# Attention's lead-in moved into the block that computes the projections, in key-chunk order, on one core

## The chip, the cores and the metric

The kernel runs on one core of a Trainium2 chip. The metric is the device time in microseconds (us) of one execution; the time before is the median of three runs. A core has five engines that work side by side: TensorE (PE in the profile; its weight loads are listed as PEld), VectorE (DVE), ScalarE (ACT), GpSimd (POOL) and SyncE (SP), which here only issues DMAs. Each engine works through its own instructions in order and waits on semaphores for the others.

## The reference, cut to what matters

The layer is an attention with a convolutional side path, a layer norm, a linear layer with fake-quantised (MXFP4) operands, and a second layer norm, on two sequences of 2048 rows of 256 features, all in float32. The change touches only the scores and what feeds them:

```python
# D, H, DK = 256, 16, 16 ; batch 2, length 2048
q_in = linear(x, Wq_w, Wq_b).transpose(0, 2, 1)
Q3 = conv1d(q_in, convq_w, convq_b, (1, 1))                 # 3 taps
Q_cat = jnp.concatenate([q_in, Q3], axis=1).transpose(0, 2, 1)
Q = linear(Q_cat, qproj_w, qproj_b)                         # 16 heads of 16; K likewise
V = linear(x, Wv_w, Wv_b)
tau = sigmoid(conv1d(gelu(conv1d(x_conv, tau1_w, tau1_b, groups=D)), tau2_w, tau2_b))
delta = ...                                                 # the same, with del1, del2
scores = einsum('bhqd,bhkd->bhqk', Q, K) / sqrt(DK)
scores = scores * tau[..., None] + delta[:, :, None, :]
attn = jax.nn.softmax(scores, axis=-1)
out = einsum('bhqk,bhkd->bhqd', attn, V)
x = layernorm(x + linear(out, out_w, out_b))
x = layernorm(x + quantised_linear(x))
```

## The kernel before, in words

The program has two blocks, one after the other; an engine enters the second block only when every engine has finished the first.

**First block: projections.** The 2 x 2048 rows are cut into eight chunks of 512 (`NCHUNK`, chunks 0 to 7). For each chunk, TensorE computes the keys (two halves `o` of 128 features, `project(n, 1, o)`, 18 matmuls each), half of the values (`values`, 12 matmuls), the queries of half 0, the other half of the values, the queries of half 1, and the pointwise convolution of the next chunk (`pointwise`, 8 matmuls, which the trace shows as 16). VectorE does the convolution taps of the next chunk, the low parts of the split of each float32 number into two, the bias of the values and the scaling of the queries with tau; ScalarE does the high parts, the GELUs and sigmoids. SyncE stores queries, keys and delta to DRAM (`k_parts`, `q_parts`, `delta_parts`). Four heads form a group; in chunks 1 to 4 SyncE also loads chunk 0 to 3 of the first group's keys and queries back into `k_set` and `q_set` (`group_load`, 14 DMAs each, semaphore `group_loaded`). It does so at its place in its queue, behind the loads of `tau_r` and ahead of the stores of the chunk's keys.

**Second block: attention.** There are 32 iterations (`NIT`): 8 groups of four heads by 4 chunks of 512 queries. An iteration needs the maximum of each query row before its softmax, and these maxima are computed one iteration ahead. They are cut into 32 units (`UNITS`): a unit is one pair of matmuls (`s_unit`, line 205) of 128 queries by 512 keys, one in each half of the array, and one VectorE reduction over the pair (`max_unit`, line 215). The units alternate between two pairs of PSUM banks, so unit s may only start on TensorE when the reduction of unit s-2 is done. When the 32 units of iteration j are done, VectorE reduces them to `nm` (line 1009), GpSimd splits `nm` in two parts, three units later TensorE transposes them (item "rows", line 800), VectorE copies them to `nm_rows` (line 998), and SyncE writes them as two extra rows into `q_set` (`rows_store`, line 785). Then the scores of iteration j are computed again, transposed, with the maximum already subtracted (`st`, line 813), ScalarE exponentiates them (line 967), and TensorE multiplies by the values (`pv_half`, line 826). The list `items` holds all units and rows in order; in steady state one slot of TensorE is one pair at line 813, eight matmuls at line 826 and mostly one item at line 205.

Before its first `st`, TensorE has to be 45 items into that list (`lead_in`): the 32 units of iteration 0, its rows item, and 12 units of iteration 1. `PRE_STEP` says how many items are done already in the first block, by chunk and by one of seven places in a chunk: 28 (`PRE`). Places 0 and 1 lie behind the key projections, 2 behind the first half of the values, 3 behind the queries of half 0, 4 behind the second half of the values, 5 behind the queries of half 1, and 6 behind the pointwise convolution. VectorE has the same seven places in its own order (`pre_max`). The other 17 items stand at the head of the second block (line 896), each followed by six matmuls whose result nobody reads (`WARM`, line 901), 102 in all.

At the end of the first block SyncE waits for the last stores and group loads (lines 334 to 337). At the start of the second, ScalarE loads the table of the exponential and GpSimd fills `v_grp`, the values of the first group.

## Time and profile before

| | |
|---|---|
| time before, median of 3 runs | 1717.49 us (1715.56 to 1720.35) |
| profiled execution: time, span of the trace | 1709.64 us, 1707.8 us |
| first block | 0 to 254.2 us |
| lead-in at the head of the second block | 254.2 to 274.4 us |
| busy: TensorE, VectorE, ScalarE, GpSimd | 96%, 90%, 78%, 4% of the span |
| granted TensorE clock, mean | 0.982 |

Times in the trace are us from the start of the span. "x" counts instructions. A bracket at the end of a timeline row is the idle time of that engine just before the row, and the instruction that ended it. PEclk is the granted TensorE clock as a share of full speed: 1.00 is 2.4 GHz, 0.50 is 1.2 GHz. Rows of a timeline that merge several instructions give the start of the first and the time to the end of the last. The ends of matmuls are modelled, so a TensorE that is 100% busy may hide short idle stretches.

### The profile page before, as it was taken

To read this page: it belongs to the slowest core of one execution; us is meant where nothing else is said; L and a number is where in the kernel's file an instruction comes from. 1 tells how busy PE (TensorE), PEld (TensorE's weight loads), DVE (VectorE), ACT (ScalarE), POOL (GpSimd) and SP (SyncE) were. 2 spreads that over 40 slices of the span, in tenths; PEclk is the share of its full clock that TensorE was granted. 3 is DMA by queue.
4 is the path that set the end of the run, shared out by engine and by line. 5 is a ranking of instruction groups with operands and counts; after the bars stand their busy time and mean duration, and the time that the engine had idled before them with its cause. 6 is when DMAs were issued, how large, how long until landed. Compare 5 with 4: busy or idle time off the path is not lost.

```text
span 1707.8 us, 33648 instructions
## 1 busy us (share of the span) xinstructions
PE 1639.0 (96%) x13978; PEld 742.4 (43%) x13978; DVE 1536.4 (90%) x1622; ACT 1325.2 (78%) x2401; POOL 74.5 (4%) x133
## 2 busy tenths in 40 slices
PE   8999989999999999999999999999999999999775
PEld 7677754333333333333333333333333333334564
DVE  5688978999999999999999999999999999973896
ACT  3788724888888888888888888888888888886333
POOL 3000002000000000000000000000000000010110
PEclk9999999999999999999999999999999999999988
DMA  3377336000600060023004100602060000002331
GB/s 110 99 183 185 106 95 91 8 8 8 83 8 9 13 78 12 10 35 57 8 8 61 34 8 8 85 9 82 8 84 8 8 8 15 8 10 55 104 123 50
DMA packets 46960, 84.72 MB, mean 50 GB/s; under 512 B 9116, under 2 KB 21020, under 8 KB 44092
## 3 DMA queue, kind: packets, MB, share of 16 engines
q1 hardware_dynamic: 44952, 82.49, 22.6%
q8 instruction: 109, 1.79, 0.5%
q14 instruction: 43, 0.35, 0.1%
q10 hardware_dynamic: 1856, 0.09, 0.1%
HBM read 51.36 MB, written 30.67 MB: 48 GB/s over the span
## 4 chain that ended last, share of the span: by engine, by line
PE 61%; DVE 22%; ACT 2%; issue 1%; ACTq 0%; POOL 0%; DVEq 0%
PE ps L826 26%; PE ps L813 20%; DVE mx L215 17%; PE ps L205 11%; PE ps L885 1%; DVE work L1052 1%; ACT y L944 1%; PE ps L901 1%; ACT o_sb L944 1%; DVE small L1047 0%; PE ps L800 0%; PE ps L891 0%; DVE stats L1026 0%; PE ps L857 0%; DVE work L1061 0%
## 5 line engine op out<-in xcount | busy, mean ns | idle before, releaser
L215 DVE TENSOR_REDUCE mx<-ps 128x2 f32<-128x1024 f32 x1024 | 1233.0, 1223 | 58.8 <-PE ps L205 49.2
L967 ACT ACTIVATE e<-ps 128x512 f32<-128x512 f32 x2048 | 1110.1, 596 | 198.7 <-PE ps L813 158.5
L826 PE MATMUL ps<-e,v_grp 128*32 128x256 f32 x8192 | 655.1, 392 | 0.5 <-ACT ev L956 0.5
L813 PE MATMUL ps<-q,k 52*128 52x512 f32 x2048 | 523.8, 497 | 3.8 <-ACT e L967 3.8
L205 PE MATMUL ps<-k,q 50*128 50x512 f32 x2048 | 420.0, 402 | 10.9 <-DVE mx L215 6.2
L813 PEld LDWEIGHTS ps<-q,k 52*128 52x128 f32 x2048 | 198.9, 183 | 429.0 <-ACT e L967 399.6
L826 PEld LDWEIGHTS ps<-e,v_grp 128*32 128x32 f32 x8192 | 161.5, 108 | 358.6 <-issue 199.4
L205 PEld LDWEIGHTS ps<-k,q 50*128 50x128 f32 x2048 | 198.0, 187 | 39.1 <-DVE mx L215 30.4
L605 PE MATMUL ps<-x_p,m_p 128*128 128x512 f32 x576 | 141.3, 401 | 0.0
L605 PEld LDWEIGHTS ps<-x_p,m_p 128*128 128x128 f32 x576 | 107.7, 190 | 30.6 <-issue 5.7
L437 DVE SCALAR_TENSOR_TENSOR hid<-x_c,dw_w,hid 128x512 f32<-128x512 f32 x128 | 88.5, 747 | 13.2 <-ACT hid L379 13.2
L385 ACT ACTIVATE hid<-hid 128x512 f32<-128x512 f32 x64 | 40.5, 632 | 41.0 <-DVE hid L437 39.5
L1026 DVE BATCH_NORM_STATS2 stats<-ps 128x6 f32<-128x256 f32 x64 | 23.2, 418 | 27.9 <-PE ps L857 18.8
L379 ACT ACTIVATE hid<-x_c,dw_b,dw_w 128x512 f32<-128x512 f32 x64 | 46.7, 804 | 0.2
L83 POOL CAST nm_pad<-nm 128x16 fp32r<-128x16 f32 x32 | 6.3, 197 | 914.9 <-DVE nm L1009 914.9
L944 ACT ACTIVATE y<-ps,shift,rstd 128x256 f32<-128x256 f32 x32 | 15.4, 563 | 24.3 <-DVE shift L1038 19.7
L857 PE MATMUL ps<-wo_t,v_all 128*128 128x256 f32 x128 | 34.2, 392 | 0.0
L883 PE MATMUL ps<-bias,ones 128*128 128x512 bf16 x16 | 8.3, 521 | 25.9 <-ACT o_sb L944 25.9
L944 ACT ACTIVATE o_sb<-ps,shift,rstd 128x256 f32<-128x256 f32 x32 | 15.4, 563 | 21.1 <-DVE shift L1038 21.1
L625 PE MATMUL ps<-hid,pw_w 128*16 128x512 f32 x128 | 31.2, 594 | 0.5 <-ACT hid L385 0.5
L428 ACT ACTIVATE q_sp<-qx 128x512 fp32r<-128x512 f32 x16 | 10.1, 630 | 26.3 <-DVE qx L465 26.2
L616 PE MATMUL ps<-wv_p,x_p 128*128 128x256 f32 x192 | 27.1, 292 | 2.0 <-DVE v_all L455 2.0
(117 smaller groups left out, 658.2 us busy)
## 6 DMA issues: line engine op xcount, KB each, us to landing
k<-k_parts SPq DMA_DIRECT2D x42, 256.0 KB
q<-q_parts SPq DMA_DIRECT2D x42, 256.0 KB
k_parts<-k_sp SPq DMA_DIRECT2D x16, 512.0 KB, 4.9
q_parts<-q_sp SPq DMA_DIRECT2D x16, 512.0 KB, 4.5
att<-ev SPq DMA_DIRECT2D x32, 256.0 KB
x_c<-in_x_t SPq DMA_DIRECT2D x8, 514.0 KB, 6.4
tau_r<-tau_rows SPq DMA_DIRECT2D x16, 256.0 KB
x_in<-in_x SPq DMA_DIRECT2D x8, 512.0 KB, 3.7
```

The lines of the kernel that those rows point to most:

```text
L205: last = nc.tensor.matmul(ps[:, s_bank(s) + half, :], q_set[r, g % 2, jh, lo + qt * P:lo + (qt + 1) * P], k_set[r, g % 2, jh, kc * CH:(kc ...
L215: nc.vector.tensor_reduce(mx[:, j % 2, :, jh, qt, kc], ps[:, b0:b0 + 2, :], AX.X, ALU.max).then_inc(s_free, 1)
L379: nc.scalar.activation(hid[:, k, c, r], x_c[:, n % 2, c, 1:1 + CH], ACT.Identity, bias=dw_b[:, k, c, r:r + 1], scale=dw_w[:, k, c, r, 1:2] ...
L385: nc.scalar.activation(hid[:, k, c, r], hid[:, k, c, r], ACT.Gelu).then_inc(gelu_done, 1)
L437: nc.vector.scalar_tensor_tensor(y_, x_c[:, n % 2, c, which:which + CH], dw_w[:, k, c, r, which:which + 1], y_, ALU.mult, ALU.add).then_in ...
L605: last = nc.tensor.matmul(ps[:, o, :], m_p[:, kw, side, c, tap, P * o:P * (o + 1)], x_p[:, n % 2, kx_, c, tap:tap + CH], start=(m == 0), s ...
L625: last = nc.tensor.matmul(ps[32 * k:32 * k + H, TD_BANK, :], pw_w[:, k, 2 * c + r, :], hid[:, k, c, r, :], start=(j < 2), stop=(j >= 6))
L813: nc.tensor.matmul(ps[:, st_bank(n), :], k_set[r, g % 2, jh, kt * P:(kt + 1) * P], q_set[r, g % 2, jh, lo:lo + CH], start=True, stop=True) ...
L826: last = nc.tensor.matmul(ps[32 * h:32 * (h + 1), 0, PVW * part:PVW * (part + 1)], v_grp[:, kt, h, :], e[:, x % E_BUFS, h * CH + PVW * par ...
L857: last = nc.tensor.matmul(dst, a_t[p][:, c, P * a:P * (a + 1)], wo_t[:, c, :], start=False, stop=(c == CT - 1))
L944: last = nc.scalar.activation(dst[:, a], tok(bank0, a), ACT.Identity, scale=rstd[:, k, p, a:a + 1], bias=shift[:, k, p, a:a + 1])
L967: nc.scalar.activation(e[:, x % E_BUFS, h * CH:(h + 1) * CH], ps[:, st_bank(n), :], ACT.Exp).then_inc(e_ready, 1)
```

## The change

All 45 items of the lead-in are now done in the first block. `PRE_STEP` gives 4 items to chunk 1 (places 3 to 6, one each), 5 each to chunks 2 to 6 (places 2 to 6), and 16 to chunk 7 (2, 2, 3, 2, 2, 2, 3). The 32 units of iteration 0 are taken in another order: by key chunk first (`place_of`), so that the first 8 need only the first key chunk; the first unit of each key chunk waits for that chunk's 14 loads. The last unit of iteration 0, `nm` and the rows item fall into chunk 7: `row_maxima`, `split_max` and `rows_store` become functions shared by both blocks and are called for iteration 0 in the first. `rows_store(sp, 0)` stands in SyncE's queue of chunk 7 behind the key stores and ahead of the delta store. The 102 matmuls at line 901 are gone. SyncE's waits for the last stores move from the end of the first block to the start of the second, ahead of the loads that follow there. The buffers that these stores read (`q_sp`, `k_sp`, `td`, `d_sp`) are allocated first, so that only buffers loaded behind these waits lie over them. The zeroing of `nm_pad` moves from VectorE to GpSimd's start.

```diff
+        def place_of(j, u):
+            if j == 0:
+                return u % (HH * TT) // HH, u % HH, u // (HH * TT)
+            return u // (HH * NQ), u // NQ % HH, u % NQ
 
         def s_unit(pe, s):
             if s >= 2:
                 pe.wait_ge(s_free, s - 1)
             g, lo = j // NQ, j % NQ * CH
-            if u == 0 and j % NQ == 0:
+            qt, jh, kc = place_of(j, u)
+            if j == 0 and (qt, jh) == (0, 0):
+                pe.wait_ge(group_loaded, 16 * GROUP_DMAS * (kc + 1))
+            if u == 0 and j % NQ == 0 and j > 0:
                 pe.wait_ge(group_loaded, loads_of(g + 1))
-            qt, jh, kc = u // (HH * NQ), u // NQ % HH, u % NQ
...
+        def rows_turn(pe, s):
+            j, u = items[s]
+            pe.wait_ge(s_free, s - 1)
+            pe.wait_ge(nm_ready, j + 1)
+            nc.tensor.transpose(ps[:, s_bank(s), 0:P], nm_pad[:].bitcast(F32), ident_f[:]).then_inc(s_full, 1)
...
-        PRE_STEP = {4: (0, 0, 0, 0, 0, 0, 2), 5: (0, 0, 1, 1, 1, 1, 1), 6: (0, 0, 1, 1, 1, 1, 1), 7: (2, 2, 2, 2, 2, 2, 4)}
+        PRE_STEP = {1: (0, 0, 0, 1, 1, 1, 1)} | {n: (0, 0, 1, 1, 1, 1, 1) for n in range(2, 7)} | {7: (2, 2, 3, 2, 2, 2, 3)}
...
+                        if n > 1:
+                            sp.wait_ge(group_loaded, 16 * GROUP_DMAS * (n - 1))
                         group_load(sp, 0, group_loaded, slice((n - 1) * CH, n * CH))
                     for o in range(CT):
                         sp.wait_ge(k_split, CT * n + o + 1)
                         store_parts(k_parts, k_sp, n, o, k_stored)
+                    if n == NCHUNK - 1:
+                        rows_store(sp, 0)
...
-                sp.wait_ge(k_stored, 16 * CT * NCHUNK)
-                sp.wait_ge(q_stored, 16 * CT * NCHUNK)
-                sp.wait_ge(d_stored, 16 * NCHUNK)
-                sp.wait_ge(group_loaded, loads_of(1))
...
                     for s in range(PRE, lead_in):
                         s_item(s)
-                        for m in range(WARM):
-                            for half in range(2):
-                                r = rows_of(half, K_S)
-                                nc.tensor.matmul(ps[:, st_bank(half), :], q_set[r, 0, 0, 0:P], k_set[r, 0, 0, 0:CH], start=True, stop=True)
...
+                    sp.wait_ge(k_stored, 16 * CT * NCHUNK)
+                    sp.wait_ge(q_stored, 16 * CT * NCHUNK)
+                    sp.wait_ge(d_stored, 16 * NCHUNK)
                     sp.dma_start(fw[:], t["ffn_w"].rearrange("(a p) i -> p a i", p=P)).then_inc(ffn_loaded, 16)
...
-                    rows_store(sp, 0)
```

TensorE in chunk 1, from its key projections to its pointwise convolution. In the rows of before, line 605 is a projection, 616 the values, 625 the pointwise convolution; `ps` is PSUM. Before:

```order
L605 MATMUL ps<-x_p,m_p 128x512 x36
L616 MATMUL ps<-wv_p,x_p 128x256 x12
L605 MATMUL ps<-x_p,m_p 128x512 x18
L616 MATMUL ps<-wv_p,x_p 128x256 x12
L605 MATMUL ps<-x_p,m_p 128x512 x18
L625 MATMUL ps<-hid,pw_w 16x512 x8
```

TensorE at the same place now; there the same three are lines 668, 679 and 688, and line 218 is the pair of a unit:

```order
L668 MATMUL ps<-x_p,m_p 128x512 x36
L679 MATMUL ps<-wv_p,x_p 128x256 x12
L668 MATMUL ps<-x_p,m_p 128x512 x18
L218 MATMUL ps<-k,q 128x512 x2
L679 MATMUL ps<-wv_p,x_p 128x256 x12
L218 MATMUL ps<-k,q 128x512 x2
L668 MATMUL ps<-x_p,m_p 128x512 x18
L218 MATMUL ps<-k,q 128x512 x2
L688 MATMUL ps<-hid,pw_w 16x512 x8
L218 MATMUL ps<-k,q 128x512 x2
```

Four units stand in chunk 1 where none stood; the first of them, behind the 18 matmuls of the queries of half 0, is the one that waits for the first 14 loads. TensorE from the first half of the values in chunk 7 to the start of the second block, before (line 205 is a unit's pair, line 901 the unread matmuls, the two branches are the border of the blocks):

```order
L616 MATMUL ps<-wv_p,x_p 128x256 x12
L205 MATMUL ps<-k,q 128x512 x4
L605 MATMUL ps<-x_p,m_p 128x512 x18
L205 MATMUL ps<-k,q 128x512 x4
L616 MATMUL ps<-wv_p,x_p 128x256 x12
L205 MATMUL ps<-k,q 128x512 x4
L605 MATMUL ps<-x_p,m_p 128x512 x18
L205 MATMUL ps<-k,q 128x512 x12
L288 UNCONDITIONAL_BRANCH
L789 UNCONDITIONAL_BRANCH
L205 MATMUL ps<-k,q 128x512 x2
L901 MATMUL ps<-k,q 128x512 x6
```

TensorE at the same place now; line 235 is the transpose of the rows item, line 859 the first scores of attention proper (line 813 before):

```order
L679 MATMUL ps<-wv_p,x_p 128x256 x12
L218 MATMUL ps<-k,q 128x512 x4
L235 MATMUL ps<-ident_f,nm_pad 128x128
L668 MATMUL ps<-x_p,m_p 128x512 x18
L218 MATMUL ps<-k,q 128x512 x4
L679 MATMUL ps<-wv_p,x_p 128x256 x12
L218 MATMUL ps<-k,q 128x512 x4
L668 MATMUL ps<-x_p,m_p 128x512 x18
L218 MATMUL ps<-k,q 128x512 x10
L343 UNCONDITIONAL_BRANCH
L837 UNCONDITIONAL_BRANCH
L859 MATMUL ps<-q,k 128x512 x8
```

The transpose stands ahead of the queries of half 0, and behind the border attention's own matmuls come first.

## Rows read from the trace of the kernel before

**Rows 1.** the profile page, part 1: busy time, share of the span, instructions.
```profile
PE 1639.0 (96%) x13978; PEld 742.4 (43%) x13978; DVE 1536.4 (90%) x1622; ACT 1325.2 (78%) x2401; POOL 74.5 (4%) x133
```

**Rows 2.** the chain that ended last, in order of time: start us, us, what.
```profile
254.24 0.79 PE ps L205 x2
...
274.45 0.59 ACT e L967
```

**Rows 3.** groups by line, 254.2 to 274.05 us: busy us, mean ns, idle before.
```profile
L215 DVE TENSOR_REDUCE mx<-ps 128x2 f32<-128x1024 f32 x16 | 18.6, 1218 | 1.8 <-PE ps L205 1.8
L901 PE MATMUL ps<-k,q 50*128 50x512 f32 x102 | 16.0, 420 | 0.0
```

**Rows 4.** busy time by stretch, chunks 4 and 6: PE, PEld, DVE, ACT, POOL, PEclk, DMA.
```profile
142.62:166.62 24.00, 24.00 (x118) 17.37 (x116) 18.88 (x31) 19.97 (x30) 0.00 (x0) 1.00 0.68 179
...
192.78:218.85 26.07, 26.07 (x124) 18.03 (x122) 24.03 (x32) 19.05 (x27) 0.00 (x0) 1.00 0.34 105
```

**Rows 5.** timeline of the ScalarE queue at the start of the second block.
```profile
254.20 1.28 ACT L967 ACT_TABLE_LOAD   x1 [5.95 <-PEq L288]
```

**Rows 6.** timeline of TensorE: where chunks 2 and 3 begin.
```profile
95.88 8.65 PE L605 MATMUL ps<-x_p,m_p 128*128 128x512 f32 x36
...
119.23 8.67 PE L605 MATMUL ps<-x_p,m_p 128*128 128x512 f32 x36
```

**Rows 7.** timeline of TensorE in chunk 1.
```profile
82.42 4.37 PE L605 MATMUL ps<-x_p,m_p 128*128 128x512 f32 x18
86.62 1.58 PE L616 MATMUL ps<-wv_p,x_p 128*128 128x256 f32 x12
```

**Rows 8.** timeline of SyncE's DMA issues in chunk 1.
```profile
88.90 0.28 SPq L166 DMA_DIRECT2D k<-delta_parts  x1
89.22 0.89 SPq L293 DMA_DIRECT2D k_parts<-k_sp  x2
```

**Rows 9.** DMA issues of 220 to 262 us.
```profile
delta_parts<-d_sp SPq DMA_DIRECT2D x1, 64.0 KB, 1.9
```

**Rows 10.** DMA issues of 84 to 90 us: count, KB, median us to landing.
```profile
k_parts<-k_sp SPq DMA_DIRECT2D x2, 512.0 KB, 5.6
```

**Rows 11.** timeline of TensorE after its idle stretch at 56 us.
```profile
57.68 2.93 PE L616 MATMUL ps<-wv_p,x_p 128*128 128x256 f32 x12 [1.98 <-DVE v_all L455]
```

**Rows 12.** timeline of VectorE in chunk 7, and the reduction to `nm`.
```profile
232.53 2.35 DVE L215 TENSOR_REDUCE mx<-ps 128x2 f32<-128x1024 f32 x2
...
248.89 4.61 DVE L215 TENSOR_REDUCE mx<-ps 128x2 f32<-128x1024 f32 x4
...
260.68 0.22 DVE L1009 TENSOR_REDUCE nm<-mx 128x16 f32<-128x64 f32 x1
```

**Rows 13.** timeline of TensorE in chunk 7.
```profile
231.29 0.50 PE L205 MATMUL ps<-k,q 50*128 50x512 f32 x2 [0.17 <-DVE mx L215]
231.73 4.47 PE L605 MATMUL ps<-x_p,m_p 128*128 128x512 f32 x18
```

**Rows 14.** waits of SyncE's queue, 240 to 260 us: us in total, times, longest.
```profile
SPq L337 <- DMA q_parts<-q_sp: 4.3, 1, 4.3
```

**Rows 15.** busy time by stretch, 280 to 282 us.
```profile
280.00:282.00 2.00, 2.00 (x14) 0.66 (x14) 1.06 (x2) 1.08 (x2) 0.00 (x0) 0.55 1.02 127
```

**Rows 16.** timeline of TensorE as attention gets going.
```profile
277.47 0.64 PE L826 MATMUL ps<-e,v_grp 128*32 128x256 f32 x8
...
282.64 0.64 PE L826 MATMUL ps<-e,v_grp 128*32 128x256 f32 x8
...
283.88 0.64 PE L826 MATMUL ps<-e,v_grp 128*32 128x256 f32 x8
```

**Rows 17.** timeline of VectorE: the first tap of chunk 6's round.
```profile
195.62 2.87 DVE L437 SCALAR_TENSOR_TENSOR hid<-x_c,dw_w,hid 128x512 f32<-128x512 f32 x4 [1.51 <-ACT hid L379]
```

**Rows 18.** timeline of ScalarE: four middles, and the end of that round.
```profile
194.77 2.94 ACT L379 ACTIVATE hid<-x_c,dw_b,dw_w 128x512 f32<-128x512 f32 x4
...
220.16 0.68 ACT L408 ACTIVATE td<-ps,pw_b 16x512 f32<-16x512 f32 x1
```

More of the change, by code:

```diff
@@ L212, in max_unit, with rows_copy, row_maxima, split_max @@
             dve.wait_ge(s_full, s + 1)
-            qt, jh, kc = u // (HH * NQ), u // NQ % HH, u % NQ
+            qt, jh, kc = place_of(j, u)
             b0 = s_bank(s)
             nc.vector.tensor_reduce(mx[:, j % 2, :, jh, qt, kc], ps[:, b0:b0 + 2, :], AX.X, ALU.max).then_inc(s_free, 1)
+        def rows_turn(pe, s):
[3 more added lines that the diff above has]
+            nc.tensor.transpose(ps[:, s_bank(s), 0:P], nm_pad[:].bitcast(F32), ident_f[:]).then_inc(s_full, 1)
+        def rows_copy(dve, s):
+            j, u = items[s]
+            dve.wait_ge(s_full, s + 1)
+            if j > 0:
+                dve.wait_ge(rows_set, j * ROWS_INC)
+            nc.vector.tensor_copy(nm_rows[:], ps[0:2 * HG * TT, s_bank(s), 0:P]).then_inc(s_free, 1)
+        def row_maxima(dve, s):
+            j, u = items[s]
+            dve.wait_ge(s_free, s + 1)
+            if j > 0:
+                dve.wait_ge(nm_ready, j)
+            nc.vector.tensor_reduce(nm[:], mx[:, j % 2].rearrange("p a j q c -> p (a j q) c"), AX.X, ALU.max, negate=True).then_inc(nm_max, 1)
+        def split_max(pool, j):
+            pool.wait_ge(nm_max, j + 1)
+            if j > 0:
+                pool.wait_ge(s_full, rows_at[j - 1] + 1)
+            cols = nm[:].rearrange("p (h q) -> p h q", h=HG)
+            high(nc.gpsimd, nm_parts[:, :, 0], cols).then_inc(nm_high, 1)
+            pool.wait_ge(nm_high, j + 1)
+            low(nc.gpsimd, nm_parts[:, :, 1], cols, nm_parts[:, :, 0]).then_inc(nm_ready, 1)
+        def rows_store(sp, j):
+            sp.wait_ge(s_free, rows_at[j] + 1)
+            g, lo = j // NQ, j % NQ * CH
+            for h in range(HG):
+                row = HALF * (h // HH) + ROW_MAX
+                sp.dma_start(q_set[row:row + 2, g % 2, h % HH, lo:lo + CH].bitcast(F32).rearrange("t (a l) -> t a l", a=TT),
+                             nm_rows[h * 2 * TT:(h + 1) * 2 * TT, :].bitcast(F32)).then_inc(rows_set, 16)
         early = top.enter_context(ExitStack())
+        q_sp = sb(early, "q_sp", [P, CT, 2, CH], F32R)
+        k_sp = sb(early, "k_sp", [P, CT, 2, CH], F32R)
+        td = sb(early, "td", [48, CH])
+        d_sp = sb(early, "d_sp", [48, 2, CH], F32R)
         x_c = sb(early, "x_c", [P, 2, CT, CH + TAPS - 1])
@@ L342, in _ @@
                 nc.gpsimd.memset(eps_col[:], EPS).then_inc(ident_ready, 1)
+                nc.gpsimd.memset(nm_pad[:].bitcast(F32), 0.0).then_inc(pad_zero, 1)
                 pool.wait_ge(ident_ready, 2)
@@ L530, in pre_max @@
                     for s in pre_at.get((n, place), ()):
+                        j, u = items[s]
+                        if u == "rows":
+                            rows_copy(dve, s)
+                            continue
                         max_unit(dve, s)
+                        if u == UNITS - 1:
+                            row_maxima(dve, s)
                 for n in range(NCHUNK):
@@ L630, in pre_scores @@
                     for s in pre_at.get((n, place), ()):
-                        s_unit(pe, s)
+                        if items[s][1] == "rows":
+                            rows_turn(pe, s)
+                        else:
+                            s_unit(pe, s)
                 beta(1, 0)
@@ L794, in s_item @@
                         j, u = items[s]
[L795 removed]
+                        if u == "rows":
+                            rows_turn(pe, s)
+                        else:
                             s_unit(pe, s)
[L797 to L800 removed]
                     def st(x, jh):
```

56 lines of the change are left out of this document (11 added, 45 removed).

## The prediction, made before the changed kernel had run

> **What bounds the kernel now.** I read the page first: TensorE is busy for 96% of the span [rows 1], so whatever takes or gives TensorE time counts unless it lies where TensorE waits. Then the chain that ended last, in order of time. From the border of the blocks it runs through the lead-in on TensorE, and 20.2 us later (254.24 to 274.45) it reaches the first exponential [rows 2]: until then nothing of attention proper is done, ScalarE stands still. The groups by line of that stretch show what fills it: 16 reductions on VectorE of 18.6 us together, and 102 unread matmuls on TensorE [rows 3]. So the lead-in is paced by both, and all of it is on the path. Last I read the first block, to which the work goes, by stretches: in chunks 4 and 6 TensorE is busy 24.00 of 24.00 and 26.07 of 26.07 us [rows 4]. TensorE bounds that block as well, and nothing moved there is free.
>
> **What goes.** With the change the second block begins with the exponential's table load of 1.28 us (254.20 to 255.48) [rows 5], beside which the first scores run; the first exponential follows at 1.3 us behind the border instead of 20.2. Removed: 18.9 us.
>
> **What the units cost in chunks 1 to 6.** A chunk without units takes 119.23 - 95.88 = 23.35 us [rows 6]; chunk 6, with five single units, 26.07, or (26.07 - 23.35) / 5 = 0.54 us a unit; chunk 4, with two units side by side, 24.00 [rows 4]. Chunk 1 gets four single units, 2.2 us; chunks 2 and 3 five each, 2 x 2.72 = 5.4; chunk 4 goes from 24.00 to 26.07, 2.1; chunks 5 and 6 are as they were. Sum 9.7 us. From below, if each cost what one of the side-by-side pair does ((24.00 - 23.35) / 2 = 0.33), chunks 1 to 3 would come to 4.6 instead of 7.6; I take the single units' price, since they stand singly. VectorE, busy for 24.03 us of chunk 6, just holds that pace; if it doesn't, that is a rival below.
>
> **The new wait in chunk 1.** This is the largest term. The first unit stands behind the queries of half 0, which end at 82.42 + 4.37 = 86.79 us; before, TensorE went straight on to the values [rows 7]. The unit waits for all 14 loads of the first key chunk. SyncE issues them at the same place as before, and nothing ahead of them changes: the last is issued at 88.90 us, 2.1 us after TensorE has arrived, and the stores of the keys follow it at once [rows 8]. When it lands the trace does not print. From below, a small transfer on a quiet queue takes 1.9 us [rows 9]: 88.90 + 0.28 + 1.9 = 91.1, a wait of 4.3 us. From above, the key stores issued from 89.22 on take 5.6 us [rows 10]; if the loads have to share the queues with them to the end, the last lands with them at 89.7 + 5.6 = 95.3, a wait of 8.5 us. I take the 5.6 us of the transfers right behind, from the last load's own issue: 88.90 + 5.6 = 94.5, a wait of 7.7 us, because the load is in the same queues in the same microseconds. Behind the waiting unit are queued the second half of the values, the queries of half 1, the pointwise convolution and all of chunk 2; VectorE waits in its turn behind the same unit with the bias of the values, four taps and the query scaling behind it. TensorE has no slack to give this back, so it stays on the path. The three later waits of this kind find their loads landed: the second key chunk is first read at the end of chunk 2, its loads are issued some ten us earlier.
>
> The Trainium skill (page "DMA: Bandwidth & Descriptors", section "Anatomy of one DMA — SWDGE (gpsimd) path") puts a transfer at a fixed 2.0 us plus its bytes over the bandwidth. For a transfer alone the trace agrees (1.9 us) [rows 9]; on the loaded queue it does not (5.6 us) [rows 10]. By that rule the wait would be about 4 us and not 7.7, which is the rival of the early landing below.
>
> **The clock.** After a standstill TensorE works at half speed for a while: behind an idle stretch of 1.98 us that ends at 57.68, the 12 matmuls of the values took 2.93 us [rows 11] instead of 1.58 [rows 7]. I expect the same behind the wait in chunk 1. For some 3.4 us at 1.2 GHz half is lost, 1.7 us; bounds 0 and 3.4.
>
> **Chunk 7.** It is paced by VectorE and by the two bank pairs. It loses one reduction: the last four start at 248.89 and take 4.61 us, 1.14 us apiece [rows 12]. It gains the reduction to `nm`, 0.22 us [rows 12], and the copy of the rows, an estimate of as much again. But the rows item stands ahead of the queries of half 0 and may start only when the unit two before it is reduced. That unit is the first of place 2, whose reduction VectorE begins at 232.53 and ends 1.2 us later (two took 2.35); with `nm` ahead, 234.0 [rows 12]. Before, the queries of half 0 began at 231.73, having waited 0.17 us [rows 13]; now they begin behind the transpose at about 234.4. From there VectorE follows TensorE (it waits for the units after each projection), so all shifts by 2.7 and the missing reduction takes back 1.1: +1.6 us. Bounds: -0.7 (only VectorE's own sum counts) and +3.
>
> **The border.** SyncE waited 4.3 us for the last query stores at the end of the first block [rows 14]; that ended with VectorE's last reduction (248.89 + 4.61 = 253.50), so removing it gives nothing by itself. Behind the border it delays only loads that nobody needs for tens of us. `rows_store` is issued in chunk 7, more than 10 us ahead of the first scores, and is off the path. GpSimd's `v_grp` is filled beside the first exponentials.
>
> **The start of attention.** Before, the first slots of attention ran partly at 1.2 GHz as well: the granted clock was 0.55 at 280 to 282 us [rows 15], and from 277.47 to 282.64 three slots took 5.17 us, where the next took 1.24 [rows 16]; that is 1.45 us above three normal ones. Now the unread matmuls are gone, and attention starts at 1.2 GHz out of the thin end of chunk 7. I take the same loss, 0 in the difference; bounds -1.4 (the clock is up before the first values) and +1.5 (twice as long low). From then on the 32 iterations are the same instructions.
>
> **The sum.** Added 9.7 + 7.7 + 1.7 + 1.6 = 20.7 us, removed 18.9: +1.8 us. On the profiled execution's 1709.64 us (span 1707.8) that is 1711.4. This execution lies 7.85 us below the median of the runs shown, so I add the difference to the median: 1717.49 + 1.8 = 1719.3 us. The gain is eaten up in the first block, mostly by one wait.
>
> **Rivals.**
> 1. *The early landing.* The loads arrive by 91.1 us, the wait is 4.3 us and the clock costs 0.9: 9.7 + 4.3 + 0.9 + 1.6 - 18.9 = -2.4, 1715.1 us. For it: the loads are issued ahead of the key stores, and the 1.9 us [rows 9]. Against it: the 5.6 us [rows 10].
> 2. *VectorE and ScalarE become the bound of chunks 2 to 4 (the slower side).* A round of them goes from the first tap of a chunk to the next: in chunk 6 from 195.62 [rows 17] to the end of the sigmoids, 220.16 + 0.68 = 220.84 [rows 18], and one ScalarE middle of 0.7 us more (four took 2.94): 25.9 us, against TensorE's 26.07. There is 0.1 us of slack, without group loads and without the extra border columns that chunks 3 and 4 have. It decides from a round longer than 26.1 us; at 27.5 us it adds 1.4 in each of chunks 2, 3 and 4: +1.8 + 4.2 = +6.0, 1723.5 us. Against it: most of the extra border work is under 0.2 us an instruction, and slack of earlier chunks has to be used up first.
> 3. *Little of it shows.* The loads land early (4.3), the clock does not fall in chunk 1, chunk 7 costs -0.7, and attention starts at full clock (-1.4): 9.7 + 4.3 - 0.7 - 1.4 - 18.9 = -7.0, 1710.5 us, faster. The wait can't be less than 2.1 us, as the last load is issued only then.
>
> **Chances.** Forecast 0.52, rival 1 0.20, rival 2 0.18, rival 3 0.10. A change of 0.3% is 5.2 us; less than that a measurement of this kernel can't tell from none. Rival 3 and a tenth of rival 1 are faster: 0.12. Rival 2 and a ninth of the forecast (a wait at its upper bound with a long clock loss) are slower: 0.24. The rest, 0.64, is no change. The range of 8 in 10 takes in rivals 1 and 2 and stops short of rival 3: 1712.5 to 1726 us.
>
> **What would show it.** Right: in chunk 1 the first pair of a unit on TensorE has an idle stretch of 7 to 8 us before it, ended by a DMA, and half-speed matmuls behind it; chunks 2, 3 and 4 take 26 us each; the queries of half 0 in chunk 7 begin 2 to 3 us late; the border of the blocks comes at about 275 us instead of 254.2; the first exponential 1.3 us behind it; the iterations take as long as before. Wrong: an idle stretch in chunk 1 of 4 us or less (rival 1), chunks 2 to 4 of 27 us or more with VectorE fully busy (rival 2), or a wait at the head of the second block for the rows, for `v_grp` or for the clock.

## The result, and the profile after

The changed kernel takes 1720.93 us (median of 20 runs, 1716.02 to 1735.77), the kernel before 1715.7 us in the same comparison (20 runs, 1709.92 to 1726.52). The ratio is 1.0046 (95% interval 1.0028 to 1.0065), which is 7.9 us more (4.8 to 11.2); the two medians alone are 5.2 us apart. The time lies in the predicted range and 1.6 us from the predicted one. But the step was forecast at +1.8 us, inside what a measurement can tell from nothing, and it is about three times that by the medians and four times by the ratio: a slower kernel, if by half a percent. That the absolute time came so close is partly luck: the forecast stood on the median of three runs, 1717.49 us, and over 20 runs the kernel before has 1715.7. The profiled executions took 1716.65 and 1709.64 us, 7.0 us apart (spans 1714.9 and 1707.8 us), and it is in them that the difference is followed below. Both lie near the lowest time of their kernel.

The first part of the page of the changed kernel, as [rows 1] of before:

```profile
PE 1635.2 (95%) x13876; PEld 735.6 (43%) x13876; DVE 1534.8 (89%) x1621; ACT 1324.4 (77%) x2401; POOL 74.5 (4%) x134
```

Here TensorE is busy for 3.8 us less with 102 instructions less, in a span that is 7.0 us longer. So the time isn't in added work but in standstills and in the speed of the clock.

The timeline of TensorE of the changed kernel, in chunk 1, in chunk 7 and at the start of attention (start us, us, instruction, count, idle before and what ended it):

```profile
82.30 4.37 PE L668 MATMUL ps<-x_p,m_p 128*128 128x512 f32 x18
94.15 0.80 PE L218 MATMUL ps<-k,q 50*128 50x512 f32 x2 [7.48 <-DMA k<-delta_parts]
94.88 2.93 PE L679 MATMUL ps<-wv_p,x_p 128*128 128x256 f32 x12
...
98.46 5.46 PE L668 MATMUL ps<-x_p,m_p 128*128 128x512 f32 x18
...
253.90 0.33 PE L235 MATMUL ps<-ident_f,nm_pad 128*128 128x128 f32 x1 [2.01 <-DVE mx L228]
253.98 6.01 PE L668 MATMUL ps<-x_p,m_p 128*128 128x512 f32 x18
...
276.49 1.19 PE L859 MATMUL ps<-q,k 52*128 52x512 f32 x3 [1.74 <-PEq L343]
...
281.08 1.08 PE L872 MATMUL ps<-e,v_grp 128*32 128x256 f32 x8
...
283.24 1.08 PE L872 MATMUL ps<-e,v_grp 128*32 128x256 f32 x8
...
285.40 1.08 PE L872 MATMUL ps<-e,v_grp 128*32 128x256 f32 x8
...
287.56 1.02 PE L872 MATMUL ps<-e,v_grp 128*32 128x256 f32 x8
...
289.18 0.64 PE L872 MATMUL ps<-e,v_grp 128*32 128x256 f32 x8
```

In chunk 1, where the values followed at once on the queries [rows 7], TensorE now stands still for 7.48 us, and the values and the queries behind it take 2.93 and 5.46 us instead of 1.58 and 4.37: the granted clock is 0.50 from 90.4 to 100.7 us, over all of the values and the first part of the queries. In chunk 7 the transpose waits 2.01 us for VectorE, where 0.17 us stood [rows 13], and the queries behind it take 6.01 us instead of 4.47. Behind the border, a slot of attention at first takes 2.16 us (it begins at 281.08, 283.24, 285.40 and 287.56), and from 289.18 us on the normal 1.24.

Chunks 2, 3 and 4 and attention's first slots by stretch (us, busy TensorE, weight loads, VectorE, ScalarE, GpSimd, granted clock, DMA share, GB/s); they answer to [rows 4, 15]:

```profile
108.26:134.34 26.08, 26.08 (x124) 18.03 (x122) 24.06 (x31) 18.46 (x26) 0.00 (x0) 1.00 0.58 149
134.34:160.46 26.12, 26.12 (x124) 18.04 (x123) 24.07 (x36) 19.12 (x29) 0.00 (x0) 1.00 0.62 156
160.46:186.53 26.07, 26.07 (x124) 18.02 (x123) 24.10 (x36) 19.15 (x29) 0.00 (x0) 1.00 0.58 156
...
281.00:288.00 7.00, 7.00 (x44) 2.29 (x44) 2.78 (x3) 3.71 (x8) 2.88 (x7) 0.50 1.06 154
```

The three chunks are TensorE's alone, as chunk 6 was. The last row is the one to remember: TensorE is busy for 7.00 of 7.00 us as far as the profile shows, and its clock is 1.2 GHz all the same.

The timeline of SyncE of the changed kernel, the last of the 14 loads and the key stores behind it ([rows 8] before); then ScalarE's at the border ([rows 5]):

```profile
88.77 0.28 SPq L166 DMA_DIRECT2D k<-delta_parts  x1
89.09 0.89 SPq L348 DMA_DIRECT2D k_parts<-k_sp  x2
```

```profile
276.45 1.28 ACT L1009 ACT_TABLE_LOAD   x1 [4.40 <-PEq L343]
277.74 2.56 ACT L1009 ACTIVATE e<-ps 128x512 f32<-128x512 f32 x5
```

The loads are issued when they were, and reach the waiting unit 5.4 us later (88.77 to 94.15). The border lies at 276.45 us, and the first exponential 1.3 us behind it.

Last, a place that is the same in all these kernels and lies behind all that was changed: VectorE's reduction to `nm` for iteration 1, and for the last iteration. In the kernel before:

```profile
305.08 0.22 DVE L1009 TENSOR_REDUCE nm<-mx 128x16 f32<-128x64 f32 x1
...
1519.90 0.22 DVE L1009 TENSOR_REDUCE nm<-mx 128x16 f32<-128x64 f32 x1
```

and in the changed kernel:

```profile
310.39 0.22 DVE L251 TENSOR_REDUCE nm<-mx 128x16 f32<-128x64 f32 x1
...
1527.19 0.22 DVE L251 TENSOR_REDUCE nm<-mx 128x16 f32<-128x64 f32 x1
```

At the first the changed kernel is 5.31 us late, at the last 7.29. So 5.3 us arise ahead of 310 us and 2.0 in the 30 iterations that are the same instructions in both; behind them 0.3 us come back, which makes the 7.0.

### The profile page after: what moved, and what is told of

It reads as the page before. It is cut to its first block, busy times and chain, and to the rows that moved or that the text cites. A ratio compares the mean times of both kernels' runs of the same rounds, so it can differ in the third digit from the quotient of the medians.

```text
span 1714.9 us, 33445 instructions
## 1 busy us (share of the span) xinstructions
PE 1635.2 (95%) x13876; PEld 735.6 (43%) x13876; DVE 1534.8 (89%) x1621; ACT 1324.4 (77%) x2401; POOL 74.5 (4%) x134
## 4 chain that ended last, share of the span: by engine, by line
PE 60%; DVE 21%; ACT 2%; issue 1%; DMA 1%; SPq 0%; ACTq 0%; POOL 0%; DVEq 0%
PE ps L872 26%; PE ps L859 20%; DVE mx L228 17%; PE ps L218 11%; PE ps L903 1%; DMA out<-o_sb 1%; PE ps L931 0%; ACT y L986 0%; PE ps L235 0%; DVE stats L1061 0%; ACT o_sb L986 0%; DVE work L1087 0%; PE ps L901 0%; DVE small L1082 0%; PE ps L937 0%
## 5 line engine op out<-in xcount | busy, mean ns | idle before, releaser
L494 DVE SCALAR_TENSOR_TENSOR hid<-x_c,dw_w,hid 128x512 f32<-128x512 f32 x128 | 88.6, 747 | 10.2 <-ACT hid L436 10.2
L442 ACT ACTIVATE hid<-hid 128x512 f32<-128x512 f32 x64 | 40.5, 632 | 57.9 <-DVE hid L494 56.5
L1061 DVE BATCH_NORM_STATS2 stats<-ps 128x6 f32<-128x256 f32 x64 | 23.1, 417 | 27.4 <-PE ps L903 18.9
L981 ACT ACTIVATE std<-mv,eps_col 128x4 f32<-128x4 f32 x16 | 4.9, 305 | 33.2 <-DVE mv L1065 27.9
L903 PEld LDWEIGHTS ps<-wo_t,v_all 128*128 128x128 f32 x128 | 27.1, 212 | 4.6
```

Source lines behind the costliest of these rows:

```text
L442: nc.scalar.activation(hid[:, k, c, r], hid[:, k, c, r], ACT.Gelu).then_inc(gelu_done, 1)
L494: nc.vector.scalar_tensor_tensor(y_, x_c[:, n % 2, c, which:which + CH], dw_w[:, k, c, r, which:which + 1], y_, ALU.mult, ALU.add).then_in ...
L903: last = nc.tensor.matmul(dst, a_t[p][:, c, P * a:P * (a + 1)], wo_t[:, c, :], start=False, stop=(c == CT - 1))
```

## The experiments

Ratios are to the kernel before, run on the same chip (its medians there: 1713.98 to 1714.96 us). Three distances are read from every trace: from the start of the queries in chunk 1 (82.42 before, 82.30 after, 82.07 to 86.41 elsewhere, since the start of the kernel varies) to the border of the blocks; from the border to the `nm` of iteration 1; and the stretch of low clock that begins at most 10 us ahead of the border or behind it and lasts beyond it.

Each trace is one execution. The times of those of e5 and e9 lie 7 and 8 us above the median of their kernels; they and those of e4 and e8 have a further stretch of low clock of 20 to 31 us at the end of attention, behind all three distances.

| kernel | queries to border | border to `nm` | low clock there | ratio |
|---|---|---|---|---|
| before | 171.78 | 50.88 | 10.2, and 3.4 | 1 |
| changed | 194.15 | 33.94 | 17.1 | 1.0046 (1.0028 to 1.0065) |
| changed, again (e10) | 191.80 | 33.83 | 17.1 | 1.0050 (1.0024 to 1.0076) |
| e1 | 182.07 | 36.61 | 23.9 | 0.9994 (0.9972 to 1.0016) |
| e2 | 189.96 | 37.64 | 23.9 | 1.0044 (1.0016 to 1.0072) |
| e3 | 194.40 | 40.08 | 23.9 | 1.0029 (1.0000 to 1.0058) |
| e4, one run | 191.89 | 36.73 | 23.9 | 1726.56 us |
| e5 | 171.75 | 55.63 | 44.4 | 1.0027 (0.9996 to 1.0057) |
| e6 | 194.95 | 30.51 | none | 1.0015 (0.9987 to 1.0044) |
| e7 | 180.02 | 30.52 | none | 0.9938 (0.9914 to 0.9962) |
| e8, one run | 187.66 | 33.88 | 17.1 | 1721.97 us |
| e9 | 180.02 | 38.46 | 27.3 | 0.9972 (0.9952 to 0.9992) |

**No wait in chunk 1 (e1).** The four units of chunk 1 move: two to its end, one more each to chunks 2 and 3.

```diff
-PRE_STEP = {1: (0, 0, 0, 1, 1, 1, 1)} | {n: (0, 0, 1, 1, 1, 1, 1) for n in range(2, 7)} | {7: (2, 2, 3, 2, 2, 2, 3)}
+PRE_STEP = {1: (0, 0, 0, 0, 0, 0, 2)} | {n: (0, 1, 1, 1, 1, 1, 1) for n in (2, 3)} | {n: (0, 0, 1, 1, 1, 1, 1) for n in (4, 5, 6)} | {7: (2, 2, 3, 2, 2, 2, 3)}
```

> The four units of chunk 1 are moved: two to place 6 of chunk 1, where the loads have landed, one more each to chunks 2 and 3 (place 1). Theory (the wait for the first 14 loads and the clock behind it are lost outright, since TensorE bounds the first block): the idle stretch of 7.5 us in chunk 1 goes, no half-speed matmuls follow, chunks 2 and 3 become 26.6 us each, the border of the blocks comes 9 to 10 us earlier than in the changed kernel (near 267 us), and the time is 9 to 10 us below it, about 2 us below the kernel before (ratio 0.998 to 1.000). Rival A (VectorE and ScalarE bound the chunks with five or six units, slack 0.1 us): chunks 2 and 3 become 27.2 us or more, with TensorE idle in them, and the border comes only 8 us earlier. Rival B (what is lost in chunk 1 is slack that chunk 7 takes back): the border moves by less than 5 us.

Measured: 1712.86 us. The timeline of TensorE in chunk 1, then chunks 2 and 3 by stretch:

```profile
90.29 1.58 PE L679 MATMUL ps<-wv_p,x_p 128*128 128x256 f32 x12
91.70 4.37 PE L668 MATMUL ps<-x_p,m_p 128*128 128x512 f32 x18
```

```profile
100.21:126.92 26.71, 26.71 (x127) 18.14 (x125) 26.10 (x33) 18.54 (x27) 0.00 (x0) 1.00 0.59 149
126.92:153.68 26.76, 26.76 (x127) 18.14 (x125) 24.87 (x37) 18.87 (x29) 0.00 (x0) 1.00 0.62 153
```

No standstill, and values and queries at full speed. Chunk 1 takes 14.13 us from its queries to chunk 2, instead of 25.96; a sixth unit in chunks 2 and 3 costs 0.6 us each, though VectorE is busy for 26.10 us of chunk 2. The border comes 12.1 us earlier than in the changed kernel's first trace and 9.7 us earlier than in its second (e10); 1.5 us of the 12.1 lie in chunk 7, where e1 happens to keep full speed. 2.7 us are given back behind the border, where the clock stays low longer (23.9 us against 17.1). The wait is the largest single cost, as the forecast had it: the interval of e1's ratio lies below that of the changed kernel, and without the wait the kernel stands level with the one before.

**The rows item a place later (e2).** In chunk 7 the transpose comes behind the queries of half 0 instead of ahead of them.

```diff
-{7: (2, 2, 3, 2, 2, 2, 3)}
+{7: (2, 2, 2, 3, 2, 2, 3)}
```

> Only the rows item of chunk 7 moves, from place 2 (ahead of the queries of half 0) to place 3 (behind them). Theory: TensorE's idle 2.0 us before the transpose goes, and with it the half-speed stretch in the queries of half 0 (6.01 us against 4.47), so the queries of half 0 begin 2 us earlier and the border comes 3 to 4 us earlier than in the changed kernel (near 273 us). Rival: chunk 7 is paced by VectorE's sum, and the border moves by less than 1 us, with VectorE's idle time merely elsewhere. Time 3 us below the changed kernel or the same.

Measured: 1723.14 us. TensorE's timeline in chunk 7:

```profile
255.32 4.49 PE L668 MATMUL ps<-x_p,m_p 128*128 128x512 f32 x18
259.65 0.27 PE L235 MATMUL ps<-ident_f,nm_pad 128*128 128x128 f32 x1
```

The standstill of 2.01 us is gone, the queries keep full speed, and chunk 7 takes 34.14 us instead of 37.73. Against the changed kernel's second trace, where the queries kept full speed too (36.16 us, e10), the new place gives 2.0 us; the rest was the clock. The border is 4.2 us earlier (1.8 against e10), and `nm` comes 3.7 us later behind it, with 23.9 us of low clock instead of 17.1: in this execution the start of attention takes what chunk 7 gives. The time doesn't move. So the standstill was real, but removing it alone gained nothing that the runs show.

**What the unread matmuls did (e5, e3, e6).** In the kernel before alone (e5) the 102 unread matmuls are left out, and nothing else:

```diff
                     for s in range(PRE, lead_in):
                         s_item(s)
-                        for m in range(WARM):
-                            for half in range(2):
-                                r = rows_of(half, K_S)
-                                nc.tensor.matmul(ps[:, st_bank(half), :], q_set[r, 0, 0, 0:P], k_set[r, 0, 0, 0:CH], start=True, stop=True)
```

> The kernel before, with only its 102 unread matmuls taken out; the 17 items stay at the head of the second block. Theory (attention's own mix of matmuls at 1.2 GHz does not reliably bring the clock back; the unread matmuls did): the clock is still at 0.5 when the first scores of attention start, stays there for 10 to 20 us more, the slots of that stretch take 2.16 us instead of 1.24, and the kernel is 4 to 9 us slower than before (ratio 1.002 to 1.005). Rival (the late recovery in the changed kernel comes from starting attention right at the border, with its loads and GpSimd's work beside it): the clock comes back within 4 us as before, and since the unread matmuls also stood in the lead-in's way, the kernel is 0 to 2 us faster than before.

Measured: 1720.38 us, its ratio just not clear of 1. Its stretches behind the border:

```profile
258.00:277.00 19.00, 12.60 (x36) 5.04 (x36) 17.65 (x19) 1.10 (x1) 14.13 (x25) 0.50 0.47 88
277.00:297.00 20.00, 19.74 (x104) 6.82 (x101) 9.72 (x9) 11.64 (x22) 0.00 (x0) 0.52 0.99 116
```

The first row is the lead-in, the second attention: TensorE is busy for 19.74 of 20.00 us and at 0.52 of its clock. The way from the border to `nm` is 4.75 us longer than before. The low clock lasts from 252.0 to 296.4 us. In the kernel before it had begun in the thin end of chunk 7 as well, at 247.7 us, but it was over at 257.9, 3.7 us behind the border, and the next fall came only at 278.4, when the unread matmuls had ended. They brought the clock back and held it, and the change took them away together with the lead-in. The 4.75 us are a balance: the first exponential comes 0.9 us earlier without them (19.4 us behind the border instead of 20.2), and the way from it to `nm` is 5.6 us longer.

In e3 the changed kernel gets unread matmuls again where TensorE would wait: 17 pairs around the last three units of chunk 7, seven between the first scores of attention.

```diff
+                def fill(bank, pairs):
+                    for m in range(pairs):
+                        for half in range(2):
+                            r = rows_of(half, K_S)
+                            nc.tensor.matmul(ps[:, bank + half, :], q_set[r, 0, 0, 0:P], k_set[r, 0, 0, 0:CH], start=True, stop=True)
...
+                        if (n, place) == (NCHUNK - 1, 6):
+                            if k == 0:
+                                pe.wait_ge(v_evac, 2 * NCHUNK)
+                                pe.wait_ge(td_ready, NCHUNK)
+                            fill(V_BANK, (3, 2, 8)[k])
...
+                        if s == PRE - 1:
+                            fill(V_BANK, 4)
...
+                            if x < AHEAD and 2 <= n < HG * AHEAD - 1:
+                                for m in range(3 if n == 2 else 1):
+                                    for other in range(2):
+                                        r = rows_of(other, K_S)
+                                        nc.tensor.matmul(ps[:, 4 + other, :], q_set[r, 0, 0, 0:P], k_set[r, 0, 0, 0:CH], start=True, stop=True)
```

> Unread matmuls are put where TensorE idles: 17 pairs at the end of chunk 7 between the last units, 7 pairs between the first scores of attention. Nothing else changes. Theory (attention starts at 1.2 GHz because TensorE was thinly used before it): the granted clock stays at 1.0 from 270 us on, the first four slots of attention take 1.24 instead of 2.16 us, and steady state is reached 3 us earlier; the time is 3 us below the changed kernel. Rival (the slow start is the wait for the exponentials, not the clock): the slots stay above 1.8 us with the clock at 1.0, and nothing is gained. A loss of 1 us would mean that the unread matmuls stand in the way of the scores.

Measured: 1724.2 us. Its timeline of TensorE at the border, and the stretch behind it:

```profile
277.02 0.69 PE L872 MATMUL ps<-q,k 52*128 52x512 f32 x3 [1.11 <-PEq L343]
...
278.92 0.79 PE L872 MATMUL ps<-q,k 52*128 52x512 f32 x1 [0.52 <-ACT e L1027]
```

```profile
280.00:300.00 20.00, 20.00 (x115) 7.21 (x111) 8.99 (x8) 10.95 (x21) 11.05 (x20) 0.50 1.00 160
```

This fill held the clock until 1.6 us behind the border (278.6 us) and lost it there, behind a standstill of 1.11 us and within one of 0.52 us. Then TensorE is busy for 20.00 of 20.00 us at 1.2 GHz. The result is the longest way to `nm` of the changed kernels in one trace, 40.08 us; neither the theory nor its rival had that. Over all runs e3 is not slower than the changed kernel (1.0029 against 1.0046, intervals overlap). The Trainium skill (page "TensorE: Matmul & The Clock Gate", section "What's actually happening") has the throttled state as the default and "activity releases the throttle". By that rule a TensorE that is always busy should come to full speed; this row, 20.00 of 20.00 us busy by the profile at a granted clock of 0.50, does not agree with it.

In e6 the same places are filled denser: `(3, 2, 9)` and 7 pairs at the end of chunk 7, five pairs instead of three behind the third of the first scores.

```diff
-                            fill(V_BANK, (3, 2, 8)[k])
+                            fill(V_BANK, (3, 2, 9)[k])
-                            fill(V_BANK, 4)
+                            fill(V_BANK, 7)
-                                for m in range(3 if n == 2 else 1):
+                                for m in range(5 if n == 2 else 1):
```

> As the kernel e3_warm, with more unread matmuls: 21 pairs at the end of chunk 7 instead of 17, 9 pairs between the first scores instead of 7, the most of them in the 1.3 us in which ScalarE loads its table. Theory (in e3_warm the clock fell 1.7 us behind the border because TensorE stood still there for 1.1 and 0.5 us; once the slots start at 2.4 GHz they hold it): the clock stays at 1.0 through the start of attention, the first slots take 1.24 us, steady state is reached 4 to 5 us earlier than in the changed kernel, the time is 4 to 5 us below it, near the kernel before (ratio 0.999 to 1.002). Rival (the border's standstill alone brings the clock down): it falls again at the same place, and the start costs what it cost in e3_warm, 6 us more than in the changed kernel.

Measured: 1716.12 us. The stretch behind its border at 280.66 us:

```profile
281.00:293.00 12.00, 11.94 (x108) 5.35 (x104) 6.60 (x6) 11.11 (x21) 7.14 (x14) 1.00 0.81 158
```

Full clock, and 30.51 us to `nm`: 3.4 us less than in the changed kernel and 9.6 less than in e3, which differs from it by six pairs. A standstill of 0.42 us is left at its border, where e3 has 1.11. The ratios of the whole kernels, 1.0015 against 1.0046, point the same way, but their intervals overlap.

**What the loads of chunk 1 wait for (e4, e8).** The forecast had the last load share the queues with the key stores issued behind it. In e4 SyncE holds these stores until all 14 loads have landed.

```diff
+                    if n == 1:
+                        sp.wait_ge(group_loaded, 16 * GROUP_DMAS)
                     for o in range(CT):
                         sp.wait_ge(k_split, CT * n + o + 1)
                         store_parts(k_parts, k_sp, n, o, k_stored)
```

> SyncE holds back the key stores of chunk 1 until the 14 loads of the first key chunk have landed; nothing else changes. Theory as in the prediction (the loads share the queues with the 1 MB of key stores issued right behind them): the loads land near 91 us instead of 94.2, TensorE's idle stretch in chunk 1 shrinks from 7.5 to 4 or 5 us. Rival (the loads' own small rows and the loads of tau_r ahead of them take that long): the stretch stays at 7 us or more, and the key stores are issued only at 94 us.

Measured: 1726.56 us, one run. The last load and the first key store in SyncE's timeline, and TensorE's unit:

```profile
92.23 0.28 SPq L166 DMA_DIRECT2D k<-delta_parts  x1
98.37 0.89 SPq L348 DMA_DIRECT2D k_parts<-k_sp  x2
```

```profile
98.40 0.80 PE L218 MATMUL ps<-k,q 50*128 50x512 f32 x2 [8.18 <-DMA k<-delta_parts]
```

With nothing issued behind it, the last load is still there only 6.1 us after its issue (92.23 to 98.37, where SyncE's wait for it ends). The stores are not what makes it late: the rival named ahead of the run was right. In e8 the loads go ahead of the two loads of `tau_r` (256 KB each, a broadcast), which stood ahead of them:

```diff
-                    sp.wait_ge(tau_stored, 16 * (n + 1))
-                    if n > 0:
-                        sp.wait_ge(q_evac, CT * n)
-                    for o in range(CT):
...
-                        sp.dma_start(tau_r[:, o], src).then_inc(tau_loaded, 16)
                     if 0 < n <= NQ:
...
                         group_load(sp, 0, group_loaded, slice((n - 1) * CH, n * CH))
+                    sp.wait_ge(tau_stored, 16 * (n + 1))
+                    if n > 0:
+                        sp.wait_ge(q_evac, CT * n)
+                    for o in range(CT):
...
+                        sp.dma_start(tau_r[:, o], src).then_inc(tau_loaded, 16)
```

> The changed kernel, with SyncE's 14 loads put ahead of its wait for the tau rows and of the two loads of tau_r (in chunks 1 to 4). Theory (e4_late has shown that the key stores behind the loads do not delay them; what does is the 512 KB of tau_r ahead of them and their own 784 KB): the last load is issued 2 us earlier and lands 3.5 to 4.5 us behind its issue instead of 5.3, so TensorE's idle stretch in chunk 1 is 4 to 5 us instead of 7.5. Rival (the loads' own rows pile up on few of the 16 DMA engines, whatever is ahead): the landing stays 5 to 6 us behind the last issue, and the stretch shrinks by the 2 us of the earlier issue alone, to 5.5 us.

Measured: 1721.97 us, one run. SyncE's timeline and TensorE's:

```profile
89.36 0.28 SPq L166 DMA_DIRECT2D k<-delta_parts  x1
89.74 1.23 SPq L382 DMA_DIRECT2D tau_r<-tau_rows  x2
```

```profile
91.22 0.50 PE L218 MATMUL ps<-k,q 50*128 50x512 f32 x2 [2.33 <-DMA k<-delta_parts]
```

Now the last load is there 1.9 us after its issue, with the 512 KB of `tau_r` issued behind it, and TensorE waits 2.33 us; theory (4 to 5) and rival (5.5) both expected more. Of the 5.15 us less than in the changed kernel 1.6 are the earlier issue and 3.5 the faster landing. So in these two single executions the landing goes with what is in the queues ahead of the loads, not with what follows them. The border comes 187.66 us behind the queries, 4.1 to 6.5 us sooner than in the two runs of the changed kernel. The time of the whole is no verdict on it: it is one run, and it has a further low-clock stretch at the end of attention.

**All of it together (e7), and without the fill (e9).** e7 is the changed kernel with the edits of e1, e2 and e6; e9 is e7 without any unread matmul. Their edits are those shown above.

> Three edits at once: chunk 1 without a waiting unit (as e1_free), the rows item behind the queries of half 0 (as e2_rows), and the unread matmuls of e6_dense. Theory (the three costs are separate and add up): the border at 180 us behind the end of chunk 1's first queries minus 2 to 4 (e1_free had it at 182), attention at full clock from its first slot, steady state 8 to 10 us earlier than in the kernel before, ratio 0.994 to 0.996. Rival (the clock falls at the border whatever is done): no better than e1_free, ratio 0.998 to 1.001.

> The kernel e7_best without its unread matmuls: chunk 1 without a waiting unit and the rows item behind the queries of half 0. Theory (the unread matmuls are what makes the start of attention run at 2.4 GHz): the border of the blocks where e7_best has it, 180 us behind the start of chunk 1's first queries, the clock at 0.5 from before the border until 10 to 20 us behind it, the reduction to nm of iteration 1 at 34 to 39 us behind the border instead of 30.8, and a time 4 to 8 us above e7_best with a wider spread of the single runs; ratio to the kernel before 0.996 to 0.999. Rival (the placing of units and rows alone makes e7_best fast, the unread matmuls change nothing): ratio 0.994, and 31 us behind the border.

Measured: e7 1704.35 us (9 runs, eight of them between 1702.51 and 1705.73), ratio 0.9938 (0.9914 to 0.9962); e9 1707.84 us, 0.9972 (0.9952 to 0.9992). e7 beats both kernels; e9 beats the changed one, and the one before by 0.3%, with the interval's end just under 1. Behind the border, e7 and then e9:

```profile
264.47:276.00 11.53, 11.42 (x98) 5.50 (x98) 5.80 (x5) 10.73 (x19) 5.58 (x11) 1.00 0.82 154
```

```profile
266.00:285.00 19.00, 19.00 (x108) 6.26 (x109) 9.46 (x8) 10.11 (x19) 10.64 (x18) 0.51 1.01 156
```

Their borders lie the same 180.02 us behind the queries; the way to `nm` is 30.52 us in the one and 38.46 in the other. That is what the fill is worth between these two executions, 7.9 us; over all runs the ratios put it at 0.34%, 5.8 us, with intervals that overlap between 0.9952 and 0.9962. So its worth over all runs is likely, not proven. e7's fill is 30 pairs, and the kernel is 10.6 us below the one before. In its trace the way from the queries of chunk 1 to `nm` is 12.1 us shorter than in the kernel before; the expectation had 8 to 10.

**The changed kernel once more (e10).**

> The changed kernel once more, unaltered, on the same chip as e9_unfilled. Theory (two costs of it vary from run to run, since it is chance how soon the clock comes back while attention runs at 1.2 GHz): the wait in chunk 1 again 7 to 8 us, the nm of iteration 1 at 34 to 39 us behind the border, ratio to the kernel before 1.003 to 1.006. Rival (its slower time was a matter of the chip or of the single profile): ratio within 1.001 of 1, nm of iteration 1 at 31 us.

Measured: 1722.7 us, ratio 1.0050 (1.0024 to 1.0076). Its trace tells what in the first one was chance. The queries of half 0 in chunk 7:

```profile
255.31 4.44 PE L668 MATMUL ps<-x_p,m_p 128*128 128x512 f32 x18
```

They keep full speed behind the same 2.01 us of standstill, and chunk 7 takes 36.16 us instead of 37.73. The wait in chunk 1 (8.13 us) and the low clock around the border (17.1 us) are there again. But the clock behind the wait costs 1.4 us here instead of 2.8. So the way from the queries of chunk 1 to `nm` is 3.0 us longer than in the kernel before, where the first trace had 5.4.

## Why the prediction was right and wrong

Each term, as forecast and as the profiled execution has it:

| term | forecast | measured |
|---|---|---|
| units in chunks 1 to 6 | 9.7 | 9.7 (2.2 of them in chunk 1 not seen apart) |
| wait in chunk 1 | 7.7 | 7.48 |
| clock behind it | 1.7 | 2.8 |
| chunk 7 | 1.6 | 2.4 |
| from the border to `nm` | -18.9 | -16.94 |
| the same 30 iterations after | 0 | 2.0 |

The forecast's column adds up to +1.8, the measured one to +7.4; the start ahead of chunk 1's queries and the end behind the last `nm` take 0.4 off, which gives the 7.0 us between the profiled executions. The chance of 0.64 stood on no change, and 0.24 on slower, which is what came.

**Right: the units' price.** Chunks 2, 3 and 4 take 26.08, 26.12 and 26.07 us, and the forecast had 26.07. Rival 2 is out: VectorE is busy for 24.1 us there and paces nothing; even with six units (e1) the chunk is TensorE's, busy for all of it.

**Right in size, wrong in reason: the wait.** 7.48 us, and 7.8 to 8.2 in e2, e3, e6 and e10, against 7.7. I had taken 5.6 us from the key stores issued behind the loads and given their company as the reason. e4 takes the company away and the landing stays at 6.1 us; e8 takes away what stood ahead and it falls to 1.9. The number came from the row nearest in time, not from the mechanism: that it fits is luck. Rival 1 was wrong for the kernel as it is; its landing of 1.9 us is right for the kernel with another order.

**Mis-sized: the clock.** The step that failed in both traces of the changed kernel is the start of attention. I wrote "I take the same loss, 0 in the difference". The 18.9 us themselves came out (the first exponential 1.3 us behind the border instead of 20.2), but from it to `nm` the changed kernel takes 2.0 us more, and 1.9 in e10, so that the 18.9 are worth 16.94. What the change did there was to remove the matmuls that brought the clock back and held it; e5 shows in the kernel before what that costs, 4.75 us in one execution. Attention starts with slots of 2.16 us. My bound, +1.5, was too narrow: against e6's 30.51 us, with the clock up, the loss is 3.4 us here, where 1.45 was assumed, and 9.6 in e3.

Behind the wait I let half of 3.4 us be lost, and named no row for the 3.4. In the first trace the low clock lasted 10.2 us (from 90.4), 6.5 of them with work in them, and that work took 2.8 us more (the sum of the chunk, 25.96 - 13.46 = 12.5 us, less the wait of 7.48 and the four units' 2.2). Reckoned the same way it is 1.4 us in e10, 1.5 in e2, 2.7 in e3 and 2.9 in e6: the term of 1.7 lies inside what one kernel does from run to run, but its reasoning was thin. The trace of before had more to say. Right behind the values of [rows 11], for the most part in the same stretch of low clock (56.5 to 63.3 us), stands:

```profile
60.41 5.68 PE L605 MATMUL ps<-x_p,m_p 128*128 128x512 f32 x18
```

That is 1.3 us more than the normal 4.37, and with the 1.35 of the values 2.7 us behind a standstill of 1.98 us.

In chunk 7 I forecast the late start (2.7 us; it was 2.4) but not that its standstill, 2.01 us, can bring the clock down: that costs 1.5 us in the first trace and nothing in e10, where chunk 7 is 0.8 us longer than before.

The runs say the same in the large. The mean granted clock of an execution has its median at 0.974 over the 20 runs of the changed kernel and at 0.979 over 79 runs of the one before that came with the experiments. Among the runs of one kernel, each 0.001 of clock less goes with 1.3 us more (changed) and 1.1 us more (before). By these slopes the 0.005 are 5.6 to 6.6 of the 7.9 us. That is a correlation, and it includes stretches that no experiment set; in which stretches of the other runs the clock was low, the traces don't say.

**Not in the forecast: 2.0 us in the same instructions.** Most iterations take 40.28 us from `nm` to `nm` in both kernels. Every fourth, where the next group's loads are under way (DMA share 0.9 to 1.1), is longer by an amount that differs from run to run: from nothing to 1.8 us. In the longest, of 42.10 us in e7, TensorE's timeline has:

```profile
606.52 0.62 PE L890 MATMUL ps<-e,v_grp 128*32 128x256 f32 x3 [1.21 <-issue]
```

It waited for nothing that the profile shows. VectorE and ScalarE then wait for TensorE. The changed kernel's profile had 2.0 us more of this than before's; e10, the same kernel, 1.2 us more, and e7 3.9. e5, which is the kernel before but for the unread matmuls, had 1.2 us more as well. So I hold its amount for chance, and the profile of before for a lucky one. Its cause is open.

**Open too:** what decides how long the clock stays low under a busy TensorE (17.1 to 44.4 us here), and the low-clock stretches of 20 to 31 us at the end of attention in e4, e5, e8 and e9. e8's order of loads together with e7's other edits wasn't tried.

## What to carry to other kernels

When idle engine time is removed, look at what the filler in it was doing: here 102 matmuls that nobody read brought TensorE's clock back and held it, and without them the start of attention took 3.4 us more than with a fill that holds it. Put the first consumer of a load where the load has surely landed (e1: the border 9.7 to 12.1 us earlier for moving four small units), and when judging a landing time look at what is in the queues ahead of it. A start-up that is busy by the profile doesn't by itself bring the clock back (e3, e9). A fill has to close the standstills on both sides of a block border: 30 pairs did here (e6, e7), 24 did not (e3), by one trace each.

## What the runs showed of the hardware that was not expected

- TensorE can be busy by the profile, which models the ends of its matmuls, and yet stay at 1.2 GHz for long: busy 20.00 of 20.00 us at a granted clock of 0.50 (e3), 19.00 of 19.00 at 0.51 (e9), 19.74 of 20.00 at 0.52 (e5). Attention that began at the low clock got the full one back only after 11.7 to 22.6 us (eight traces); with the fill that held it, the same mix ran at 1.00 from the start (e6, e7).
- The clock fell 1.6 us behind a standstill of 1.11 us, within one of 0.52 us (e3). One of 2.01 us was followed by the fall in one execution (6.01 us for the queries) and not in another (4.44 us) of the same kernel. It stands at the same place in seven traces: the fall came in four (changed, e3, e6, e8: 6.00 to 6.02 us) and not in three (e1, e4, e10: 4.44 to 4.48 us).
- 14 loads of one key chunk landed 5.4 to 6.1 us behind the issue of the last one with 512 KB of broadcast loads ahead of them, and 1.9 us with these behind them (e8, one execution).
